# Where VectorE inverts the softmax sums inside a batch element, and where TensorE ranks the tokens: cross-attention with a routed feed-forward layer, Trainium2

## The chip, the cores and the metric

The kernel runs on one core of one Trainium2 chip. The metric is the device time of one execution in microseconds (us), median of the runs shown. Data is float32; the products are made of three products of rounded and rest parts (high x high, high x low, low x high), which TensorE takes as fp32r.

## The reference, cut to what matters

Eight batch elements of 112 tokens of width 512 attend, with 16 heads of 32, to 375 context rows: the first 257 are image rows and the last 118 are text rows, each with its own keys, values and softmax. Then a feed-forward layer of 8 experts follows, of which each token takes its two best.

```python
def attention(q, k, v):
    scores = jnp.einsum('bqhd,bkhd->bhqk', q, k) * scale
    probs = jax.nn.softmax(scores, axis=-1)
    return jnp.einsum('bhqk,bkhd->bqhd', probs, v)

q     = rms_norm(linear(x, q_w, q_b), norm_q_w)                  # x is layer-normed
k     = rms_norm(linear(ctx_txt, k_w, k_b), norm_k_w)
k_img = rms_norm(linear(ctx_img, k_img_w, k_img_b), norm_k_img_w)
x1    = x + linear(attention(q, k_img, v_img) + attention(q, k, v), o_w, o_b)
gate  = softmax(layernorm(x1) @ Wg + bg); topv, topi = top_k(gate, 2)
out   = x1 + sum over the two experts of topv * (gelu(gelu(h @ W1 + b1) @ W2 + b2) @ W3 + b3)
```

## The kernel before, in words

**Bodies and slots.** The five engines (and SyncE for the transfers) run programs of their own, tied by semaphores. After a start (`first()`) come nine bodies b = 0 to 8. Body b attends element b (`has_heads`, b up to 7), prepares queries, keys and values of element b + 1 (`has_prep`, b up to 6), projects and norms element b - 1 (`has_tail`, from b = 1) and routes element b - 2 (`has_route`, from b = 2). b = 7 is LAST, b = 8 is DONE. Then the experts run in blocks of 256 and 128 rows. A body is a loop over 16 slots h, written out in Python for each engine (`body`, lines 1009, 710, 560 and 1332): what an engine does in a slot is an `if` in that list, and the order of the ifs is the order of its queue. Nothing is reordered later, so an instruction that waits holds back all that stands behind it.

**Attention of a head.** Every fourth slot TensorE makes the scores of four heads (`score`, 12 matmuls at L1281). VectorE takes their maxima (`maxima`, L897 and L898, two pairs). ScalarE exponentiates head h in slot h with the row sums beside it (`weigh`, L658 and L660). VectorE inverts the two sums of head h - 1 in slot h (`invert_sums`, L900: a reciprocal at L904 of 112x2 numbers, then a product at L906 over the 118 text columns). ScalarE multiplies the 257 image columns in slot h (`normalise(b, h - 1)`, L666), and waits for the reciprocal alone. TensorE transposes head h - 2 in slot h (`transpose`, L1291, waits for both products and for the bank), ScalarE copies the result out (`take_transposed`, L674). In slots 6, 10, 14 and 2 of the next body TensorE multiplies four heads with the values (`attend`, L1314), and VectorE takes the sum (`attended`, L912).

**Around it, on VectorE.** `normalise_keys` (L836, L837, 257 and 118 columns), `normalise_queries` (L873), the rest parts of keys and queries (`split_keys_low` L887, `split_queries_low` L891) and of the context (`split_ctx_low` L813: 1032 columns in slot 15, 472 in slot 1), key biases (`take_kx` L861), the rest of x (`take_x` L851), layer norms (L816, L819, L823), and the gate: `gate_weights` (L927 to L931, slot 1), `gate_choice` (L936 to L946, slot 2; it ends with the mask `msk`), `gate_slots` (L951 to L955, slot 3).

**On GpSimd.** Rounded parts: `split_queries` (L466), `split_keys` (L459), both of the next element in slot 14 and right behind them `split_ctx_high` (L476, 1032 columns, which waits until ScalarE has taken the values tile v1 out, L641); `attended_high` (L470), x + bias (L577, slot 3), squares (L452), and `scatter` (two indirect DMAs, L534, slot 4).

**On TensorE.** Large products fill each slot (`FILL`): k (L1176 to L1178), kt and qt (L1241 to L1243), v (L1258 to L1260), o (L1265 to L1267). `rank` (L1329, L1330) counts, from `msk`, how many tokens before a token chose the same expert; it stands in slot 3 between the transpose and the second half of kt. It writes the bank pvb, which `gate_slots` must have read (`rank_read`) before the transposes kx (L1203, slot 4) write it. Those need `take_kx` before the transposes xT (L1203, slot 5) write the same bank, and these need `take_x` before attend. The logits (L1360, slot 15) need the `attended` of slot 14, and the second half of v2 stands behind them.

```python
if h == 0 and has_tail(b):          # VectorE, L1013
    invert_sums(b - 1, NH - 1)
if h and has_heads(b):
    invert_sums(b, h - 1)
if h == (6 if fixed(b, DONE) else 3) and has_route(b):   # TensorE, L1362
    pe.wait_ge(S["a_done"], NC * b)
    rank(b - 2)
```

## Time and profile before

| | |
|---|---|
| time, median of 3 runs | 835.34 us (834.56 to 838.92) |
| the profiled execution's own time | 834.9 us |
| its span | 832.7 us |
| busy share: TensorE, VectorE, ScalarE, GpSimd | 93%, 72%, 59%, 29% |
| mean granted TensorE clock | 0.982 |
| start | up to 39 us |
| bodies 0 to 8 | about 39 to 400 us |
| experts | the rest |
| ScalarE waiting for reciprocals (L666 for L904) | 60.6 us in 60 waits |

How to read it: in the page and the views times are us from the start of the span. A row of the timeline is start, duration, engine, line, operation, output<-input, and in brackets how long the engine sat idle before it and what ended that. PE is TensorE's matmuls, PEld its weight loads, DVE VectorE, ACT ScalarE, POOL GpSimd. PEclk is the granted TensorE clock as a part of 2.4 GHz. The spans of matmuls are modelled at their ends, so two that run one behind the other overlap a little in the rows.

### The profile page before, as it was taken

The page shows a single profiled execution, that of the slowest core. Times are in us where ns is not written, and L with a number is a line of the kernel's source. Part 1 is how long each engine was busy: PE and PEld are TensorE (multiplying, and loading weights), DVE is VectorE, ACT ScalarE, POOL GpSimd, SP SyncE. Part 2 cuts the span into 40 slices and gives each one's busy share as a digit, 9 for nine tenths or more (in the row PEclk, how much of TensorE's full clock was granted, in tenths as well). Part 3 has the DMA queues.
Part 4 walks back from the last instruction along what each step waited for, and adds up shares of the span by engine and source line. Part 5 has one row for each costly group of instructions (what it writes and reads, how often), then busy time and mean ns, then how long its engine had stood idle before and what let it go on. Part 6 is the DMA issues. An engine that isn't in the chain of part 4 may idle for free.

```text
span 832.7 us, 17460 instructions
## 1 busy us (share of the span) xinstructions
PE 770.6 (93%) x5995; PEld 666.4 (80%) x5995; DVE 599.6 (72%) x1269; ACT 490.9 (59%) x1136; POOL 240.4 (29%) x302
## 2 busy tenths in 40 slices
PE   4889898999999989787899999999999999999994
PEld 3667676767676767555798999999999999999993
DVE  6767878787978787776676757676676758676664
ACT  4377777767676777786245555554545555554543
POOL 3523334342434333223300505032140505032010
PEclk9989999999999999999999999999999999999998
DMA  9820102011020201142756665748566665648561
GB/s 308 291 83 4 56 6 58 38 35 61 24 72 13 83 13 35 31 175 89 260 203 223 233 232 208 248 172 285 191 248 220 238 233 210 250 172 286 194 220 64
DMA packets 29205, 126.28 MB, mean 152 GB/s; under 512 B 4204, under 2 KB 4220, under 8 KB 19424
## 3 DMA queue, kind: packets, MB, share of 16 engines
q1 hardware_dynamic: 23696, 109.80, 37.6%
q0 software_dynamic: 5456, 15.81, 5.3%
q8 instruction: 29, 0.48, 0.2%
q14 instruction: 24, 0.20, 0.1%
HBM read 108.42 MB, written 18.74 MB: 153 GB/s over the span
## 4 chain that ended last, share of the span: by engine, by line
PE 71%; DVE 11%; ACT 10%; issue 4%; DMA 1%; POOL 0%; SPq 0%; ACTq 0%; DVEq 0%; POOLq 0%
PE tiles L1176 6%; PE tiles L1178 6%; PE tiles L1177 6%; PE scores L1478 4%; PE scores L1480 4%; PE scores L1479 4%; PE ptb L1291 4%; PE pvb L1178 3%; PE pvb L1177 3%; PE ptb L1177 3%; PE pvb L1176 3%; PE ptb L1176 3%; PE ptb L1178 3%; PE scores L1281 2%; ACT scr L658 2%
## 5 line engine op out<-in xcount | busy, mean ns | idle before, releaser
L920 DVE TENSOR_TENSOR w<-scr,w 128x2048 fp32r<-128x2048 f32 x75 | 170.8, 2288 | 59.5 <-ACT w L684 59.5
L684 ACT ACTIVATE w<-scr 128x2048 fp32r<-128x2048 f32 x76 | 144.8, 1909 | 54.8 <-PE scores L1480 54.8
L514 POOL DMA_INDIRECT out_dram<-scr,tok x17 | 18.0, 1058 | 298.7 <-DVE scr L1155 296.2
L666 ACT ACTIVATE scr<-scr,rsum 112x257 f32<-112x257 f32 x128 | 66.7, 521 | 60.6 <-DVE rsum L904 60.6
L1176 PE MATMUL tiles<-w 128*128 128x256 f32 (+1 forms) x288 | 82.9, 288 | 0.6
L1176 PE MATMUL tiles<-c,w 128*128 128x258 f32 (+2 forms) x272 | 79.3, 291 | 2.6 <-DVE c L1129 1.2
L1177 PE MATMUL tiles<-w 128*128 128x256 f32 (+1 forms) x288 | 81.2, 282 | 0.0
L1178 PE MATMUL tiles<-w 128*128 128x256 f32 (+1 forms) x288 | 81.2, 282 | 0.0
L1143 DVE CAST w<-scr 128x256 fp32r<-128x256 f32 (+1 forms) x144 | 41.9, 291 | 52.5 <-ACT scr L774 52.5
L1178 PE MATMUL tiles<-c,w 128*128 128x258 f32 (+2 forms) x272 | 76.9, 283 | 0.0
L1177 PE MATMUL tiles<-c,w 128*128 128x258 f32 (+2 forms) x272 | 76.7, 282 | 0.0
L1291 PE MATMUL ptb<-ident,scr 112*128 112x112 f32 x384 | 61.6, 270 | 15.1 <-ACT scr L674 14.0
L1291 PEld LDWEIGHTS ptb<-ident,scr 112*128 112x128 f32 x384 | 43.0, 143 | 39.6 <-ACT scr L666 24.1
L674 ACT ACTIVATE scr<-ptb 128x336 f32<-128x336 f32 x128 | 57.7, 451 | 24.7 <-PE ptb L1291 24.6
L774 ACT ACTIVATE scr<-tiles,b12s 128x256 f32<-128x256 f32 (+1 forms) x72 | 32.3, 460 | 60.6 <-PE tiles L1178 60.5
L658 ACT ACTIVATE scr<-scores,nmax 112x257 f32<-112x257 f32 x128 | 62.5, 488 | 5.2 <-DVE nmax L898 5.2
L1145 DVE TENSOR_TENSOR w<-scr,w 128x256 fp32r<-128x256 f32 (+1 forms) x144 | 59.4, 413 | 5.0
L1176 PEld LDWEIGHTS tiles<-w 128*128 128x128 f32 x288 | 55.1, 191 | 3.3 <-DVE w L1145 2.3
L897 DVE TENSOR_REDUCE nmax<-scores 112x2 f32<-112x514 f32 x64 | 43.9, 686 | 19.1 <-PE scores L1281 19.1
L1176 PEld LDWEIGHTS tiles<-c,w 128*128 128x128 f32 x272 | 52.0, 191 | 4.4 <-issue 3.3
L1177 PEld LDWEIGHTS tiles<-w 128*128 128x128 f32 x288 | 55.2, 192 | 0.0
L1178 PEld LDWEIGHTS tiles<-w 128*128 128x128 f32 x288 | 55.2, 192 | 0.0
(223 smaller groups left out, 2332.0 us busy)
## 6 DMA issues: line engine op xcount, KB each, us to landing
scr<-in_dram SPq DMA_DIRECT2D x76, 1024.0 KB, 4.9
scr<-in_dram SPq DMA_DIRECT2D x8, 750.0 KB, 4.6
scr<-slots_d SPq DMA_DIRECT2D x10, 528.0 KB, 5.4
scr<-in_dram SPq DMA_DIRECT2D x10, 512.0 KB, 8.8
slots_d<-rows SPq DMA_DIRECT2D x8, 528.0 KB, 11.1
xn<-in_dram SPq DMA_DIRECT2D x9, 256.0 KB
xb<-in_dram SPq DMA_DIRECT2D x8, 224.0 KB, 2.7
xr<-in_dram SPq DMA_DIRECT2D x8, 224.0 KB, 2.6
```

What stands on the lines that cost most here:

```text
L658: act.activation(probs[0:L, s, 0:IMG], scores[0:L, s, 0:IMG], ACT.Exp, bias=nmax[0:L, g, s, 0:1], accum_out=sums[0:L, g, s, 0:1])
L666: act.activation(probs[0:L, s, 0:IMG], probs[0:L, s, 0:IMG], ACT.Copy, scale=rsum[0:L, g, s, 0:1]).then_inc(S["normal_img"], 1)
L674: act.activation(probT[:, h % 8, :, :], ptb[:, 0:KT * L].rearrange("p (t q) -> p t q", t=KT), ACT.Copy).then_inc(S["pt_done"], 1)
L684: act.activation(EH[slot], raw[slot], ACT.Copy).then_inc(S["eh_done"], 1)
L897: dve.tensor_reduce(of[:, :, 0], scores[0:L, 2 * i:2 * i + 2, 0:IMG], AX.X, ALU.max, negate=True)
L920: dve.tensor_tensor(EL[slot], raw[slot], EH[slot].bitcast(F32), ALU.subtract).then_inc(S["el_done"], 1)
L1143: dve.tensor_copy(hH[lay][:, c, 0:n], gel[:, m % 4, 0:n]).then_inc(S["hh_done"], 1)
L1145: dve.tensor_tensor(hL[lay][:, c, 0:n], gel[:, m % 4, 0:n], hH[lay][:, c, 0:n].bitcast(F32), ALU.subtract).then_inc(S["hl_done"], 1)
L1176: pe.matmul(out, wh, xh, start=start, stop=False)
L1177: pe.matmul(out, wh, xl, start=False, stop=False)
L1178: return pe.matmul(out, wl, xh, start=False, stop=stop)
L1291: mm = pe.transpose(ptb[:, t * L:(t + 1) * L], probs[0:L, h % 4, t * P:(t + 1) * P], ident[0:L, 0:L])
```

## The change

VectorE's `invert_sums` leaves its fixed place (head h - 1 at the head of slot h). Heads 0, 4, 8, 9 and 12 keep slot and place; the others go earlier: 1 to the end of slot 1's products (behind the low half of the context), 2 into slot 2 behind `attended`, 3 to the head of slot 3, 5 into slot 5 between `take_kx` and `take_x`, 6 into slot 6 ahead of `attended`, 7 into slot 6 behind `take_o`, 10 into slot 10 ahead of the squares, 11 to the head of slot 11, 13 into slot 13 between `normalise_queries` and `normalise_keys`, 14 into slot 14 behind `attended`, and 15 into slot 15 between `ln_apply` and `split_ctx_low` instead of the next body's slot 0. `gate_slots` goes from slot 3 to slot 4 behind the maxima, TensorE's `rank` in slot 3 behind the second half of kt (in DONE both stay), and GpSimd's `scatter` from slot 4 to slot 5. No instruction is added or taken out, and ScalarE's program is untouched.

```diff
+INVERT_FIRST = {1: 0, 3: 3, 5: 4, 9: 8, 10: 9, 11: 11, 13: 12}
+INVERT_MIDDLE = {6: 6, 10: 10}
@@ gpsimd, body @@
-                    if h == (8 if fixed(b, DONE) else 4) and has_route(b):
+                    if h == (8 if fixed(b, DONE) else 5) and has_route(b):
...
                         scatter(b - 2)
@@ vector, body @@
-                    if h == 0 and has_tail(b):
-                        invert_sums(b - 1, NH - 1)
-                    if h and has_heads(b):
-                        invert_sums(b, h - 1)
+                    if h in INVERT_FIRST and has_heads(b):
+                        invert_sums(b, INVERT_FIRST[h])
                     if h % 4 == 0 and has_heads(b):
                         maxima(b, h // 4, 0)
                         maxima(b, h // 4, 1)
...
                     if h in KEYS_LOW_AT and has_heads(b):
                         split_keys_low(b, p, KEYS_LOW_AT[h])
+                    if h in INVERT_MIDDLE and has_heads(b):
+                        invert_sums(b, INVERT_MIDDLE[h])
...
                     if h in (7, 11, 15) and has_heads(b):
                         attended_low(b, (h - 7) // 4)
+                    if h == 14 and has_heads(b):
+                        invert_sums(b, 14)
                     if h in KEYS_AT and (has_prep if h > 1 else has_heads)(b):
...
                     if h == 2 and has_tail(b):
                         attended(b - 1, 3)
+                    if h == 2 and has_heads(b):
+                        invert_sums(b, 2)
...
                     if h == 1 and has_prep(b):
                         split_ctx_low(b + 2, 1)
+                    if h == 1 and has_heads(b):
+                        invert_sums(b, 1)
                     if h == 5 and has_prep(b):
                         take_kx(b, p)
+                    if h == 5 and has_heads(b):
+                        invert_sums(b, 5)
+                    if h == 5 and has_prep(b):
                         take_x(b)
                     if h == 6 and has_tail(b):
                         take_o(b)
+                    if h == 6 and has_heads(b):
+                        invert_sums(b, 7)
+                    if h == 6 and has_tail(b):
...
                         ln_stats(b, x1, st2, mv2, "ln2")
...
                     if h == 13 and has_prep(b):
                         normalise_queries(b, p)
+                    if h == 13 and has_heads(b):
+                        invert_sums(b, 13)
+                    if h == 13 and has_prep(b):
                         normalise_keys(1 - p, 0)
...
                     if h == 15 and has_prep(b + 1):
                         ln_apply(b + 3, xb[0:L, :], xb, mv1, rs1, "ln1", "xn_done")
+                    if h == 15 and has_heads(b):
+                        invert_sums(b, 15)
+                    if h == 15 and has_prep(b + 1):
                         split_ctx_low(b + 3, 0)
...
-                    if h == (7 if fixed(b, DONE) else 3) and has_route(b):
+                    if h == (7 if fixed(b, DONE) else 4) and has_route(b):
                         gate_slots(b - 2)
@@ tensor, body @@
-                    if h == (6 if fixed(b, DONE) else 3) and has_route(b):
+                    if h == 6 and fixed(b, DONE):
                         pe.wait_ge(S["a_done"], NC * b)
                         rank(b - 2)
...
                     if b in BUSY_AT and h in BUSY_AT[b]:
                         keep_busy(tile_use("o", DONE if fixed(b, LAST) else LAST)[0], BUSY_AT[b][h])
+                    if h == 3 and has_route(b) and not fixed(b, DONE):
+                        pe.wait_ge(S["a_done"], NC * b)
+                        rank(b - 2)
```

## Rows read from the trace of the kernel before

**Rows 1.** Waits from 75 to 400 us: us in total, times, longest.
```profile
ACT scr L666 <- DVE rsum L904: 58.3, 57, 2.2
```

**Rows 2.** Windows: slots 12 to 15 of bodies 1 to 4. Busy us per engine, then granted clock, DMA.
```profile
114.59:126.43 11.84, 10.77 (x91) 7.91 (x90) 9.82 (x30) 8.45 (x28) 4.47 (x7) 1.00 0.04 4
157.84:170.85 13.01, 11.93 (x89) 8.56 (x88) 10.99 (x32) 8.46 (x28) 4.47 (x7) 0.90 0.06 20
201.87:214.60 12.73, 11.65 (x89) 8.33 (x89) 10.71 (x31) 8.45 (x28) 4.46 (x7) 0.92 0.06 21
245.86:258.27 12.41, 11.35 (x90) 8.14 (x90) 10.39 (x31) 8.45 (x28) 4.47 (x7) 0.95 0.07 20
```

**Rows 3.** Timeline of body 3, TensorE, slots 3 to 5.
```profile
178.73 0.45 PE L1291 MATMUL ptb<-ident,scr 112*128 112x112 f32 x3
...
179.68 0.33 PE L1329 MATMUL pvb<-msk,upper 112*112 112x8 f32 x2 [0.50 <-issue]
...
181.62 0.78 PE L1281 MATMUL scores<-kq 32*112 32x376 f32 x12
...
184.06 0.57 PE L1203 MATMUL pvb<-ident,xn 118*128 118x118 f32 x4
...
185.95 0.57 PE L1203 MATMUL pvb<-ident,xb 112*128 112x112 f32 x4 [0.32 <-DVE scr L861]
```

**Rows 4.** Timeline of body 3, VectorE and GpSimd, slots 2 to 4.
```profile
178.81 0.57 DVE L940 TENSOR_TENSOR sel<-tif,iota 112x16 f32<-112x16 f32 x1
179.41 0.17 DVE L946 TENSOR_TENSOR msk<-sel 112x8 f32<-112x8 f32 x1
...
179.52 1.29 POOL L577 TENSOR_TENSOR xr<-xr,obr 112x512 f32<-112x512 f32 x1
...
179.69 1.20 DVE L906 TENSOR_SCALAR scr<-scr,rsum 112x118 f32<-112x118 f32 x1
...
183.97 0.39 DVE L898 TENSOR_REDUCE nmax<-scores 112x2 f32<-112x236 f32 x1
```

**Rows 5.** Timeline of bodies 2 and 3, slots 13 to 15, TensorE, ScalarE and GpSimd.
```profile
165.37 0.50 POOL L459 CAST kq<-scr 128x376 fp32r<-128x376 f32 x1 [0.20 <-DVE scr L837]
165.42 0.51 ACT L666 ACTIVATE scr<-scr,rsum 112x257 f32<-112x257 f32 x1 [1.36 <-DVE rsum L904]
...
166.16 0.59 ACT L641 ACTIVATE scr<-tiles 128x512 f32<-128x512 f32 x1
...
166.41 0.48 PE L1291 MATMUL ptb<-ident,scr 112*128 112x112 f32 x3 [0.54 <-ACT scr L674]
...
166.89 1.05 POOL L476 CAST c<-scr 128x1032 fp32r<-128x1032 f32 x1 [1.01 <-ACT scr L641]
...
167.33 0.92 PE L1360 MATMUL pvb<-wgs,xr 128*112 128x8 f32 x8 [0.44 <-DVE af L912]
```

**Rows 6.** Timeline of body 2, slots 13 to 15, VectorE.
```profile
164.68 0.63 DVE L837 SCALAR_TENSOR_TENSOR scr<-scr,vec,rms 128x118 f32<-128x118 f32 x1
...
166.40 0.54 DVE L887 TENSOR_TENSOR kq<-scr,kq 128x376 fp32r<-128x376 f32 x1
...
166.86 0.32 DVE L912 TENSOR_SCALAR af<-pvb,vbias 128x112 f32<-128x112 f32 x1
...
167.11 1.11 DVE L836 SCALAR_TENSOR_TENSOR scr<-scr,vec,rms 128x257 f32<-128x257 f32 x1
```

**Rows 7.** Timeline of body 1, slot 3, GpSimd and VectorE.
```profile
93.09 1.31 POOL L577 TENSOR_TENSOR xr<-xr,obr 112x512 f32<-112x512 f32 x1
93.16 1.37 DVE L916 TENSOR_TENSOR a<-af,a 128x112 fp32r<-128x112 f32 x1 [0.89 <-POOL a L470]
```

**Rows 8.** Timeline of the start of body 2, TensorE.
```profile
127.82 0.36 PE L1176 MATMUL tiles<-c,w 128*128 128x258 f32 x1 [0.18 <-DVE c L813]
```

**Rows 9.** Timeline of LAST (body 7), slots 7 and 8.
```profile
362.20 0.45 PEld L1281 LDWEIGHTS scores<-kq 32*112 32x112 f32 x12 [0.36 <-issue]
...
362.98 0.51 ACT L666 ACTIVATE scr<-scr,rsum 112x257 f32<-112x257 f32 x1 [1.57 <-DVE rsum L904]
...
363.79 0.68 DVE L897 TENSOR_REDUCE nmax<-scores 112x2 f32<-112x514 f32 x1
```

## The prediction

> **What bounds the kernel now.** I read the waits of the bodies first. ScalarE stands 58.3 us for reciprocals in 57 waits, 2.2 us at most [rows 1]. That is idle time of ScalarE and not time of the kernel, so for each such wait I went to TensorE's timeline and asked whether TensorE stood too. It mostly did not: slots 8 to 11 run with large products back to back. Where it stands in a body, few things are the cause: the rank in slot 3, and in slots 14 and 15 first the transpose and then the logits. I read the rank in body 3: the transpose of slot 3 starts at 178.73, the rank only at 179.68, since its mask starts at 179.41 [rows 3, 4]. In slot 15 the transpose comes at 166.41 (0.54 idle, an ACT copy that came after a late reciprocal) and the logits at 167.33 (0.44 idle, for `attended`) [rows 5]. Then the windows: slots 12 to 15 take 11.84 us where the clock stays at 1.00, and 13.01, 12.73 and 12.41 where the mean falls to 0.90, 0.92 and 0.95 [rows 2]. In those windows the clock went to its lower level, 1.2 GHz, behind these two pauses. Bodies 5 and 6 end like body 1. So a body is TensorE's work, two or three pauses and sometimes a clock that falls; its start hangs on VectorE's queue, which is full from slot 13 on.
>
> **The change part by part.** All sums are against the profiled execution, 834.9 us with a span of 832.7, 0.44 below the median of 835.34.
>
> *Rank, slots 2 to 4.* With the rank behind kt, kt's second half follows the transpose. The time from 178.73 to the scores at 181.62 is 2.89 us [rows 3], of which transpose, kt and rank are 0.22, 1.55 and 0.38 by their starts (an estimate from the starts in this timeline); so 0.73 is pause. All of it goes if the mask is ready at 180.5. I think it is not quite. The reciprocals of heads 1 and 2 now stand ahead of the gate's choice, and `sel`, a small product of two tensors in SBUF, comes some 0.6 later than 178.81 [rows 4]. There it meets GpSimd's 1.29 us sum L577, as head 2's product does now, which took 1.20 instead of its 0.28 [rows 4]. ScalarE's earlier copy of k1 starts GpSimd 0.4 earlier, so L577 ends at 180.42; sel and mask follow, the rank at 180.8, the scores at 181.2. Gain 0.45; bounds 0.1 (both late) and 0.73. One thing is given back: kx must wait until `gate_slots` has read the rank, and that is now behind the maxima. The last of them starts at 183.97, 2.35 behind the scores [rows 4], and the read ends at +2.9; kx now starts at 184.06, +2.44 [rows 3]. So kx waits 0.48. Most of it is absorbed in the pause that xT has anyway for `take_kx` (0.32 idle, at 185.95 [rows 3]); `take_kx` comes 0.11 later. Net -0.34, in bodies 2 to 6: **-1.7**. The other side of `scatter` in slot 5, two indirect DMAs behind the squares of kx, costs nothing: its slots are read after the bodies; cover gone, it would cost GpSimd some 2 us in slot 6.
>
> *Slots 5 to 12.* ScalarE's multiplications of heads 6, 7, 10 and 11 come 1 to 2 us earlier and ScalarE waits for TensorE's next scores instead. TensorE gains nothing. Head 10's reciprocal now stands ahead of the squares and waits for its exponentials about as long as the squares wait for GpSimd: +0.05 in seven bodies, **+0.35**. Bounds 0 and +0.3 each.
>
> *Slots 13 to 15.* This is the large term. Today the keys' last product ends at 165.31, GpSimd's high part of them runs from 165.37 while VectorE does head 13, and GpSimd then idles 1.01 us until ScalarE has copied v1 out, which starts at 166.16; its 1.05 us cast of the context comes at 166.89, when the low part of the keys (166.40) is done and `attended` has begun (166.86) [rows 5, 6]. What that cast holds up is the next key product: 1.11 instead of 0.48 [rows 6]. In the new order head 13 goes ahead of the keys. ScalarE has its reciprocal 0.95 earlier than at 165.42 [rows 5], copies v1 out 0.95 earlier, and GpSimd's cast is no longer short of v1. The keys come 0.4 later, so their high part runs at about 166.2 to 166.65, and the cast follows on GpSimd at once, while VectorE only now learns that it may make the low part. There is a row of just this: the product L916 waited for GpSimd's cast L470, the next GpSimd sum started at 93.09, VectorE at 93.16, and it took 1.37 us instead of some 0.27 [rows 7]. So the low part ends at 168.0 instead of 166.94, `attended` starts 1.04 later, and the logits with it: TensorE's earlier transpose only lengthens the pause ahead of them, from 0.54 and 0.44 to one of 2.3.
>
> The rule behind this is in the Trainium skill, "SBUF — State Buffer", section "Who interferes with whom": an instruction of VectorE with two SBUF inputs and one of GpSimd that reads SBUF lock each other out, the first to issue keeps the ports to its end. By it the low part L887, which no row shows held up, is held up as L916 is; without it this term would be about +0.3. Rows 7 agree (1.37 us).
>
> Part of it comes back: the key product behind is no longer held up by the cast (0.63), but head 15 now stands ahead of the low context (+0.38). The first k product of the next body waits for that low context already now, 0.18 idle at 127.82 [rows 8], and so goes with it. The maxima stood behind the low context and head 15 and now behind the low context alone. I make the first exponentials of the next body 0.5 later: +0.5 in bodies 1 to 5, +0.7 behind body 0, and +0.3 behind body 6, which has no context to cast: **+3.5**. Bounds per body +0.2 (the cast misses) and +1.04 (nothing comes back).
>
> *LAST.* Without large products a late reciprocal counts. Its rank comes 0.45 earlier as above. Head 6 waits 1.57 us behind the layer norm, and the maxima of heads 8 and 9 start at 363.79 behind heads 6 and 7, though the scores are made from 362.20 on and could be read 0.83 later as in other slots [rows 9]; both heads move ahead, and the maxima start 0.84 earlier in all. **-0.85**; bounds -0.3 and -1.8.
>
> *Clock.* A fall costs 0.6, 0.9 and 1.2 us against 11.82 [rows 2], 0.9 in the mean. Three of six ends had one with pauses of some 1.0; with 2.3 I take two more: **+1.8**; bounds -2.7 (none is left) and +2.7.
>
> Sum: -1.7 + 0.35 + 3.5 - 0.85 + 1.8 = +3.1, so 838.0.
>
> **The rivals.** *Nothing in the way* (no change). The low part of the keys gets in ahead of the cast, and the ends of the bodies cost 0.2 instead of 0.5, with no new fall: -1.7 + 0.35 + 1.0 + 1.0 - 0.85 = -0.2, 834.7. For it: 0.1 us decides who is first; against it: rows 7, where GpSimd was. 0.20.
>
> *The pauses go* (faster). The mask is there at 180.5 and the rank gives 0.62 net, `attended` keeps its time, and the three falls vanish with the shorter pauses: -3.1 - 0.85 - 2.7 = -6.6, 828.3. For it: all sums are ready when they are now inverted. Against it: the logits wait for `attended`, not for a reciprocal. 0.17.
>
> *The logits take the blow* (slower). Place: slot 15 of bodies 1 to 5. The 1.04 us stays whole, since TensorE's v2 stands behind the logits, and all six ends fall to the lower clock: -1.7 + 0.35 + 5 x 1.04 + 1.0 - 0.85 + 2.7 = +6.7, 841.6. It decides from 0.7 us more per end than I take. Against it: the maxima of the next body have slack today of half a microsecond. 0.20.
>
> That the change only moves idle time of ScalarE, and so does nothing, comes to 834.9 and lies in the first case.
>
> **How the numbers follow.** Forecast 0.43, its own range 835 to 840. Half a per cent is 4.2 us, about what a measurement of this kernel can tell from no change. Faster than that: most of the third case, 0.16. Slower: the fourth and a little of the forecast's tail, 0.22. The rest, 0.62. The range of 8 in 10 runs from 831 into the fast case to 842.
>
> **What would show it.** In the changed profile: waits of L666 for L904 well under 30 us; the transpose of slot 3 followed by kt and the rank by the scores, 2.4 instead of 2.9 us apart; kx idle for about 0.5 behind DVE pick; the k low part L887 of slot 14 at 1.4 us or more with L476 beside it; one pause of 2 us ahead of the logits; four or five windows at the lower clock. Wrong would be: L887 at 0.54 everywhere and `attended` no later behind `normalise_queries` than now.

## The result: 1% slower, outside the range

| | before | after |
|---|---|---|
| median of 6 runs | 834.95 us (833.1 to 838.92) | 845.18 us (841.85 to 846.75) |
| ratio | | 1.0097 [1.0073, 1.0121] |
| the profiled execution's own time | 834.9 us | 845.31 us |
| mean granted TensorE clock | 0.982 | 0.968 |

Forecast 838.0, range 831 to 842. The direction of the sum was right, its size was not, and the case that the prediction called "The logits take the blow" (841.6, chance 0.20) had the place right. The page of the changed kernel begins:

```profile
span 843.4 us, 17460 instructions
...
PE 778.9 (92%) x5995; PEld 675.1 (80%) x5995; DVE 603.8 (72%) x1269; ACT 489.4 (58%) x1136; POOL 242.2 (29%) x302
```

TensorE does the same 5995 matmuls and is busy 8.3 us longer than before (770.6), at the lower mean clock of the table. Its idle time grew by 2.4 us.

Waits of the changed kernel from 75 to 400 us (us in total, times, longest):

```profile
ACT scr L669 <- DVE rsum L907: 32.4, 35, 1.8
...
PE pvb L1381 <- DVE af L915: 12.5, 6, 2.2
...
PEld pvb L1224 <- DVE pick L954: 3.6, 5, 0.7
...
DVE kq L890 <- POOL kq L462: 2.8, 7, 0.4
```

(L669 for L907 was L666 for L904 before; lines of VectorE moved by 3, of TensorE by 21.) The change did what it says: ScalarE's wait for reciprocals fell from 58.3 us [rows 1] to 32.4 (the prediction had said well under 30). No stretch of the table below got clearly shorter by it. In its place the logits (L1381) wait 12.5 us for `attended`, 2.2 in each of bodies 1 to 5 and 1.41 in body 6. Before, these six waits were 2.6 together. The wait of L890 for GpSimd (L462) occurs at seven body ends, 0 to 6.

Windows of slots 12 to 15, bodies 1 to 6 (busy us per engine, then granted clock, DMA share, GB/s):

```profile
117.73:130.63 12.90, 10.58 (x89) 7.99 (x89) 10.10 (x31) 8.36 (x28) 4.41 (x7) 1.00 0.01 4
161.47:176.32 14.85, 12.53 (x89) 9.43 (x88) 11.20 (x31) 8.45 (x28) 4.41 (x7) 0.85 0.07 17
207.28:220.59 13.31, 10.99 (x89) 8.12 (x88) 10.51 (x31) 8.46 (x28) 4.41 (x7) 0.96 0.06 18
251.58:264.81 13.23, 10.92 (x89) 8.06 (x88) 10.43 (x31) 8.45 (x28) 4.42 (x7) 0.97 0.06 13
295.79:308.90 13.11, 10.80 (x90) 7.99 (x90) 10.32 (x31) 8.45 (x28) 4.41 (x7) 0.98 0.05 11
339.83:351.90 12.07, 10.56 (x90) 7.99 (x89) 8.04 (x27) 8.45 (x28) 3.19 (x5) 1.00 0.04 7
```

The first row is body 1 at full clock: 12.90 against 11.84 [rows 2], the wait alone. The last is body 6, also at full clock: 12.07 against 11.82. In bodies 2 to 5 a fall of the clock comes on top and runs on into the next body. How the wait arises stands in the timeline of body 3, slots 14 and 15, and the start of body 4:

```profile
214.66 0.59 ACT L644 ACTIVATE scr<-tiles 128x512 f32<-128x512 f32 x1
...
215.15 0.45 PE L1312 MATMUL ptb<-ident,scr 112*128 112x112 f32 x3
...
215.21 0.83 POOL L462 CAST kq<-scr 128x376 fp32r<-128x376 f32 x1 [0.79 <-DVE scr L840]
...
215.99 1.04 POOL L479 CAST c<-scr 128x1032 fp32r<-128x1032 f32 x1
216.07 1.36 DVE L890 TENSOR_TENSOR kq<-scr,kq 128x376 fp32r<-128x376 f32 x1 [0.39 <-POOL kq L462]
217.35 0.32 DVE L915 TENSOR_SCALAR af<-pvb,vbias 128x112 f32<-128x112 f32 x1
...
217.82 0.92 PE L1381 MATMUL pvb<-wgs,xr 128*112 128x8 f32 x8 [2.22 <-DVE af L915]
...
219.15 0.39 PE L1281 MATMUL tiles<-w,c 128*119 128x512 f32 x1
...
220.04 0.63 PE L1281 MATMUL tiles<-w,c 128*119 128x512 f32 x1
```

v1 is copied out (L644) before GpSimd is done with the keys, so its context cast L479 follows at once at 215.99, and VectorE's low part, which waited for the keys' high part, comes 0.08 later and takes 1.36 us instead of 0.54 [rows 6]. `attended` (L915) then waits, and the two pauses of 0.54 and 0.44 [rows 5] are one of 2.22. Behind it the clock falls to 1.2 GHz at 219.8: the same large matmul (L1281) goes from 0.39 to 0.63 us. The 1.36 is there at six body ends, those of bodies 0 to 5, in both profiles of the changed kernel. Body 6 has no context to cast: there L890 takes 0.55 and the logits have one pause of 1.41. An L890 that is held up by the cast is what the Trainium skill, "SBUF — State Buffer", section "Who interferes with whom", says of two inputs of VectorE beside a reading GpSimd; the trace agrees (1.36 us beside the cast, 0.55 without).

**Where the 10 us are.** Time from one scores row to another, with the time at the lower clock (granted 0.50) between 75 and 425 us. "Again" is a second profile of the same kernel, on another chip; the other rows are experiments that follow.

| profile, us | bodies 0, 1 | bodies 2 to 6 | LAST, slots 0 to 11 | at lower clock |
|---|---|---|---|---|
| before | 87.0 | 217.8 | 25.7 | 17 |
| before, again | 87.1 | 218.0 | 28.5 | 27 |
| after | 91.2 | 221.3 | 28.6 | 41 |
| after, again | 89.8 | 221.5 | 28.5 | 38 |
| e1, head 13 back | 88.8 | 217.8 | 29.4 | 31 |
| e2, head 13 alone | 91.3 | 222.6 | 26.4 | 34 |
| e3, rank alone | 87.1 | 215.7 | 28.2 | 24 |
| e4, filled | 88.5 | 218.1 | 27.3 | 14 |
| e5, cast later | 90.8 | 221.8 | 29.0 | 41 |
| e14, cast later, filled | 88.9 | 216.1 | 25.7 | 17 |
| e7, before, filled | 87.9 | 216.6 | 28.3 | 17 |
| e9, rank and heads 6, 7 | 87.4 | 212.6 | 27.5 | 24 |
| e10, e9 filled | 87.6 | 212.4 | 28.5 | 17 |
| e13, e9 with heads 1, 2 | 87.1 | 216.0 | 29.1 | 27 |
| e11, e9 filled behind | 87.8 | 211.3 | 26.6 | 10 |
| e12, LAST filled too | 87.0 | 211.4 | 24.8 | 7 |

### The profile page after: what moved, and what is told of

It reads as the page before. It is cut to its first block, busy times and chain, and to the rows that moved or that the text cites. A ratio compares the mean times of both kernels' runs of the same rounds, so it can differ in the third digit from the quotient of the medians.

```text
span 843.4 us, 17460 instructions
## 1 busy us (share of the span) xinstructions
PE 778.9 (92%) x5995; PEld 675.1 (80%) x5995; DVE 603.8 (72%) x1269; ACT 489.4 (58%) x1136; POOL 242.2 (29%) x302
## 4 chain that ended last, share of the span: by engine, by line
PE 72%; DVE 12%; ACT 8%; issue 3%; DMA 2%; POOL 1%; SPq 0%; ACTq 0%; DVEq 0%; POOLq 0%
PE tiles L1197 7%; PE tiles L1199 6%; PE tiles L1198 6%; PE scores L1504 4%; PE scores L1503 4%; PE scores L1502 4%; PE ptb L1312 4%; PE pvb L1199 3%; PE pvb L1198 3%; PE ptb L1198 3%; PE pvb L1197 3%; PE ptb L1197 3%; PE ptb L1199 3%; PE scores L1302 3%; PE pvb L1335 2%
## 5 line engine op out<-in xcount | busy, mean ns | idle before, releaser
L669 ACT ACTIVATE scr<-scr,rsum 112x257 f32<-112x257 f32 x128 | 67.7, 529 | 33.2 <-DVE rsum L907 33.2
L1197 PE MATMUL tiles<-c,w 128*128 128x258 f32 (+2 forms) x272 | 81.3, 299 | 3.9 <-DVE c L816 1.8
L1198 PE MATMUL tiles<-c,w 128*128 128x258 f32 (+2 forms) x272 | 78.4, 288 | 0.0
L1199 PE MATMUL tiles<-c,w 128*128 128x258 f32 (+2 forms) x272 | 78.3, 288 | 0.0
L1312 PE MATMUL ptb<-ident,scr 112*128 112x112 f32 x384 | 63.6, 277 | 8.7 <-ACT scr L677 6.6
L1312 PEld LDWEIGHTS ptb<-ident,scr 112*128 112x128 f32 x384 | 45.0, 147 | 31.8 <-ACT scr L669 13.0
L1197 PEld LDWEIGHTS tiles<-c,w 128*128 128x128 f32 x272 | 53.9, 198 | 5.5 <-issue 3.6
L1197 PEld LDWEIGHTS tiles<-w 128*128 128x128 f32 x288 | 55.1, 191 | 3.3 <-DVE w L1166 2.3
L455 POOL TENSOR_TENSOR scr<-scr 128x257 f32<-128x257 f32 (+1 forms) x40 | 29.6, 743 | 89.9 <-ACT scr L653 57.4
L1198 PEld LDWEIGHTS tiles<-w 128*128 128x128 f32 x288 | 55.2, 192 | 0.0
## 6 DMA issues: line engine op xcount, KB each, us to landing
slots_d<-rows SPq DMA_DIRECT2D x8, 528.0 KB, 11.6
```

What stands on the lines that cost most here:

```text
L669: act.activation(probs[0:L, s, 0:IMG], probs[0:L, s, 0:IMG], ACT.Copy, scale=rsum[0:L, g, s, 0:1]).then_inc(S["normal_img"], 1)
L1197: pe.matmul(out, wh, xh, start=start, stop=False)
L1198: pe.matmul(out, wh, xl, start=False, stop=False)
L1199: return pe.matmul(out, wl, xh, start=False, stop=stop)
L1312: mm = pe.transpose(ptb[:, t * L:(t + 1) * L], probs[0:L, h % 4, t * P:(t + 1) * P], ident[0:L, 0:L])
```

## The experiments

Each run is compared with runs of the kernel before on the same chip. In none is any of the computation left out; "filled" ones have idle matmuls more, whose products nobody reads.

**e1: head 13 goes back behind the keys.** The whole change but one entry.

```diff
-INVERT_FIRST = {..., 13: 12}
+INVERT_FIRST = {..., 13: 12, 14: 13}
@@ slot 13 @@
-                    if h == 13 and has_heads(b):
-                        invert_sums(b, 13)
```

> The changed kernel with head 13 alone put back to the head of slot 14, behind the first key product. Theory A (the early head 13 lets GpSimd's context cast run right behind its key cast, so VectorE's low part of the keys is locked out, the logits come 1 us later, and the longer pause brings the clock down): the low part of the keys in slot 14 is back at 0.54 us from 1.36, the logits start some 40.5 us behind the body's first scores instead of 41.5, there are no more falls of the clock than before the change, and the time is 832 to 836. Theory B (the cost lies in the other moves: head 15 ahead of the context's low part, the rank and kx): the time stays above 841. In between, 837 to 841, both have a share.

840.87 us, ratio 1.0026 [1.0009, 1.0043]. The time lies between the two theories, where both have a share. The low part of the keys is back to 0.54 at all ends, and the logits come 9.49 us behind the scores of slot 12 (after: 10.54, before: 9.49). Three ends have a fall (bodies 2, 3 and 6), as many as before. Slots 0 to 3 of a body with a start at full clock take 11.02 us where before took 10.99: of the rank's gain nothing is left. Bodies 0 and 1 still take 1.8 us more than before, though the low part of the keys is not late. The first k product of body 1 waits in one long pause, and the clock falls at 89.6 behind it:

```profile
88.17 0.36 PE L1194 MATMUL tiles<-c,w 128*128 128x258 f32 x1 [1.82 <-DVE c L816]
```

**e2: head 13 alone**, in the kernel before.

```diff
-                    if h and has_heads(b):
+                    if h and h != 14 and has_heads(b):
                         invert_sums(b, h - 1)
@@ slot 13, between normalise_queries and normalise_keys @@
+                    if h == 13 and has_heads(b):
+                        invert_sums(b, 13)
```

> The kernel before with one thing changed: head 13 is inverted between the queries and the keys in slot 13. Theory A: the low part of the keys takes about 1.36 us, the logits start 1 us later, and the time is 840 to 846, since this alone carries the loss. Theory B: within 2 us of before, 833 to 837.

847.9 us, 1.0116 [1.0095, 1.0137], above the 840 to 846 that were expected. One reciprocal and its product, moved ahead of two keys' products, cost as much as the whole change. The low part takes 1.36 us at the ends of bodies 0 to 5 and 0.55 at that of body 6, and the clock falls at four of six ends. Slots 0 to 3 of body 5, which starts at full clock, take 10.45 us instead of 10.99: half a microsecond of the late logits comes back though the rank stands where it stood.

**e3: the rank alone**, with `gate_slots` and `scatter`; no reciprocal moves.

```diff
-                    if h == (7 if fixed(b, DONE) else 3) and has_route(b):
+                    if h == (7 if fixed(b, DONE) else 4) and has_route(b):
                         gate_slots(b - 2)
@@ tensor, body; the old place of rank is kept for DONE alone @@
...
@@ tensor, body, behind kt of slot 3 @@
+                    if h == 3 and has_route(b) and not fixed(b, DONE):
+                        pe.wait_ge(S["a_done"], NC * b)
+                        rank(b - 2)
```

> The kernel before with only the rank, gate_slots and scatter moved as in the change. Theory A: the rank part is a small gain; the mask is there at its old time, so nearly all of the 0.73 us pause goes and 0.1 to 0.5 comes back at kx: 831 to 834. Theory B: kx behind the maxima gives it all back and more, 836 to 840.

838.03 us, 0.9989 [0.997, 1.0008]. The second scores come 0.8 us earlier, but slots 8 to 11 take 10.66 instead of 9.99: the transpose of head 6 now waits 0.6 for its reciprocal, which stands behind the layer norm in slot 7. Half a gain, handed back four slots later.

**e4: nine idle matmuls ahead of the logits**, in the changed kernel: the wait stays, the pause goes.

```diff
+                    if h == 15 and has_tail(b) and has_prep(b):
+                        bank, cnt = tile_use("k0" if has_prep(b + 1) else "o", b + 1)
+                        pe.wait_ge(tile_free[bank], cnt)
+                        keep_busy(bank, 9)
```

> The changed kernel with nine 512-column matmuls into a free bank between the transpose and the logits of slot 15, bodies 1 to 6; they do no work for the output and fit into the pause of about 2.4 us. Theory A with the clock as its second step: the waits stay (logits 41.5 us behind the first scores), the clock does not fall behind them, and the time drops from 845 to 836 to 840. Rival C (the wait for the logits costs the time and the clock costs next to nothing): 843 to 846.

843.47 us, 1.007 [1.0042, 1.0097]; the profiled execution, at 840.41, is the fastest of four (granted clock 0.986, the others 0.976 to 0.981). In it there is no fall in bodies 2 to 6, slots 12 to 15 take 12.90 in bodies 2 to 5 (12.53 in body 6), and each of bodies 2 to 5 takes 43.67 to 43.73. A body of before without a fall takes 42.95 or 43.04, so the wait costs 0.65 a body by itself (1.06 in slots 12 to 15, of which some 0.45 comes back in slots 0 to 3). The median lies in the range that was named for the clock costing next to nothing, and it gained only 0.3% on the changed kernel, inside the two intervals: this run shows what the wait costs, not what the clock costs.

**e5: GpSimd's context cast one slot later**, behind `attended_high`.

```diff
-                    if h == 14 and has_prep(b + 1):
+                    if h == 15 and has_prep(b + 1):
                         split_ctx_high(b + 2, 0)
```

> The changed kernel with every inversion where the change put it, and only GpSimd's context cast of slot 14 moved behind attended_high of slot 15, so that it can no longer follow the key cast at once. Theory A (the lock-out by that cast): the low part of the keys in slot 14 is back at 0.54 us, the logits start within 0.5 us of where they did before the change (40.4 to 41.0 behind the first scores), and the ratio to before is 0.997 to 1.004. Theory B (what costs is that head 13 stands ahead of the keys and delays their chain by itself): the logits stay a full microsecond late and the ratio stays at 1.007 or more.

845.45 us, 1.0083 [1.0045, 1.0122], a miss: 0.997 to 1.004 was expected. Its timeline, end of body 3:

```profile
213.61 0.83 POOL L462 CAST kq<-scr 128x376 fp32r<-128x376 f32 x1 [0.79 <-DVE scr L840]
...
214.47 0.55 DVE L890 TENSOR_TENSOR kq<-scr,kq 128x376 fp32r<-128x376 f32 x1 [0.39 <-POOL kq L462]
...
215.42 0.92 PE L1381 MATMUL pvb<-wgs,xr 128*112 128x8 f32 x8 [1.41 <-DVE af L915]
215.56 1.87 POOL L479 CAST c<-scr 128x1032 fp32r<-128x1032 f32 x1
```

The low part takes 0.55 again and the logits are 9.74 behind the scores of slot 12, 0.25 later than before: the wait is gone, the time is not. The window of slots 12 to 15 of body 3 (body 2 takes 13.10 too):

```profile
205.68:218.78 13.10, 11.59 (x89) 8.54 (x88) 10.30 (x31) 8.46 (x28) 5.24 (x7) 0.91 0.07 20
```

The clock falls to 1.2 GHz at every end of bodies 2 to 6, in the profile for 3.41 us from 172.2, 216.6, 260.9, 305.3 and 349.7. At the end of body 1 there is the same pause (1.42) and no fall. The pauses of before, 0.54 and 0.44 with matmuls between them, are together 0.98; here there is one of 1.41.

**e14: e5 with five idle matmuls in that pause**, as in e4 but `keep_busy(bank, 5)`.

> The changed kernel with the context cast of GpSimd put behind attended_high of slot 15 (as in the run of the cast put later, which took VectorE's context copy back to 0.55 us, put the logits only 0.25 us later than before, and was still 0.8% slower, with the clock at .50 for 3.41 us at every body end), and 5 idle matmuls of TensorE between the transposition of slot 15 and the logits, where its one pause of 1.41 to 1.45 us was. If the falls of the clock are what it lost: no fall at the ends of bodies 1 to 6, last quarters of about 12.1 us, bodies of 43.0 to 43.4 us, and 0.998 to 1.003 of the time of before. If the loss is a wait of the new order that has nothing to do with the clock: the bodies stay at 44 us or more and the ratio at 1.006 or more.

838.1 us (12 runs), 1.0021 [1.0011, 1.0032]. The profiled execution, at 835.08, is the fastest of the twelve. Its window of body 3:

```profile
202.67:214.74 12.07, 11.74 (x96) 8.81 (x95) 9.32 (x29) 7.94 (x27) 5.24 (x7) 1.00 0.04 9
```

Nothing else was touched, no end has a fall, the logits are as far behind the scores as in e5 (9.73), and bodies went from 44.36 to 43.2 us. So most of what e5 lost at its ends was the clock, shown by this pair: some 1.15 us for a fall of 3.41. (The texts before e14 and a0 call L890 the context copy; it is the low part of the keys.)

**a0: the changed kernel again**, unedited, on e14's chip.

> The changed kernel, not edited, profiled a second time on another chip. If its falls of the clock come from its order of work: a fall at five or six of the ends of bodies 1 to 6, as in the first profile, a span of 840 to 846 us, the context copy of slot 14 on VectorE at 1.36 us at every body end. If their number was the chance of one profile: three or four of the ends, as in the two profiles of the kernel before, and a span of 836 to 840 us.

843.98 us, span 841.9. L890 takes 1.36 at the ends of bodies 0 to 5 again. The clock falls at 88.7, 170.6, 218.4, 262.8, 307.1 and 354.9, in the first profile at 86.7, 172.0, 219.8, 264.2, 308.5 and 356.3: at the start of body 1, at the ends of bodies 2 to 5, and in slots 0 to 3 of LAST. That is four of six ends both times, the one of body 2 for 6.83 us, and not five or six. The kernel before, profiled again (b0, below), had falls at three of six ends, as the first time, but not at the same three. So the places of the falls are this order's, and not the luck of one profile. That it has more of them at the ends rests on four against three.

**e7: the kernel before, filled**: two idle matmuls ahead of the transpose of slot 15 and two ahead of the logits.

```diff
+                    if h == 15 and has_tail(b) and has_prep(b):
+                        bank, cnt = tile_use("k0" if has_prep(b + 1) else "o", b + 1)
+                        pe.wait_ge(tile_free[bank], cnt)
+                        keep_busy(bank, 2)
@@ behind the transpose @@
+                    if h == 15 and has_tail(b) and has_prep(b):
+                        keep_busy(tile_use("k0" if has_prep(b + 1) else "o", b + 1)[0], 2)
```

> The kernel before with two idle matmuls ahead of the transpose and two ahead of the logits of slot 15, in bodies 1 to 6, inside the two pauses of TensorE; nothing else. If the falls of the clock at the ends of bodies come from these pauses, they are gone and their 0.6 to 1.2 us each with them: ratio 0.994 to 0.998. If they come from something else, or the fillers get in the way: 0.999 to 1.003.

836.4 us, 0.9997 [0.9978, 1.0015]. No fall in bodies 1 to 6, but slots 12 to 15 take 12.57 each: the first filler waited 0.92 to 0.94 us for ScalarE (L641) to free the bank. Clock gained, wait added.

**e9: the parts that should pay**: the rank as in e3, and heads 6 and 7 as in the change, ahead of `attended` and of the layer norm. All other heads as before.

```diff
-                    if h and has_heads(b):
+                    if h and h not in (7, 8) and has_heads(b):
                         invert_sums(b, h - 1)
@@ slot 6, ahead of attended @@
+                    if h == 6 and has_heads(b):
+                        invert_sums(b, 6)
@@ slot 6, behind take_o @@
+                    if h == 6 and has_heads(b):
+                        invert_sums(b, 7)
```

> The kernel before with the rank part of the change and, of the inversions, only heads 6 and 7 early (slot 6). The trace of the rank part alone showed the second scores 0.8 us earlier in a body and then 0.69 us lost at the transpose of head 6, whose reciprocal stands behind the layer norm. Theory A: with head 6 early that loss is gone, slots 8 to 11 take 9.99 us again, a body is 0.5 us shorter, LAST about 0.8: ratio 0.993 to 0.997. Theory B (the gain is taken back elsewhere): 0.998 to 1.002.

832.05 us, 0.9952 [0.9937, 0.9967]: faster than before. Slots 0 to 3 take 9.91 to 10.45 (10.15 where the clock stays up), slots 8 to 11 10.0. Slot 3 of body 4 (its scores start at 211.59), TensorE and GpSimd:

```profile
220.45 1.30 POOL L577 TENSOR_TENSOR xr<-xr,obr 112x512 f32<-112x512 f32 x1
...
221.34 0.27 PE L1334 MATMUL pvb<-msk,upper 112*112 112x8 f32 x2
...
221.74 0.78 PE L1286 MATMUL scores<-kq 32*112 32x376 f32 x12
```

The rank has no idle time ahead of it. Its mask was ready at 220.50, when L577 had only begun.

**e13: e9 with heads 1 and 2 early as in the change.**

```diff
-                    if h and h not in (7, 8) and has_heads(b):
+                    if h and h not in (2, 3, 7, 8) and has_heads(b):
                         invert_sums(b, h - 1)
@@ slot 2, behind attended @@
+                    if h == 2 and has_heads(b):
+                        invert_sums(b, 2)
@@ slot 1, behind split_ctx_low @@
+                    if h == 1 and has_heads(b):
+                        invert_sums(b, 1)
```

> The kernel with the rank part and heads 6 and 7 early (e9_rank_and_6_7), and heads 1 and 2 early as well, as the change has them, ahead of the gate's weights and choice. Theory A (they push the gate's mask behind the second half of kt, so the rank waits again): the pause ahead of the rank, gone in e9, is back at 0.5 us or more, the first quarter of a body is 10.5 us or more instead of 10.0 to 10.2 where the clock stays up, and the ratio to before is 0.998 to 1.002 against 0.995 for e9. Theory B (the two heads cost nothing): like e9, 0.993 to 0.997.

837.38 us, 1.0008 [0.9989, 1.0027]: the gain of e9 is gone, and slots 0 to 3 take 10.97 to 10.99 where the body starts at full clock. Slot 3 of body 4 (scores at 213.60):

```profile
222.06 1.29 POOL L577 TENSOR_TENSOR xr<-xr,obr 112x512 f32<-112x512 f32 x1
...
222.14 1.24 DVE L938 CAST tif<-topi 112x2 f32<-112x2 uint32 x1
...
223.41 0.41 DVE L940 TENSOR_TENSOR sel<-tif,iota 112x16 f32<-112x16 f32 x1
223.85 0.17 DVE L946 TENSOR_TENSOR msk<-sel 112x8 f32<-112x8 f32 x1
...
224.12 0.33 PE L1338 MATMUL pvb<-msk,upper 112*112 112x8 f32 x2 [0.60 <-issue]
```

Two reciprocals with their products ahead of the gate's choice bring its cast `tif` beside L577, where it takes 1.24 us instead of 0.17. So `sel` starts behind the end of L577, and the rank waits 0.60 again.

**e10: e9 with e7's fillers.**

> The one before with the four idle matmuls of slot 15 as well. If the two gains are independent, both ratios multiply: 0.988 to 0.995. If the clock falls elsewhere instead, it is no better than without them.

832.75 us, 0.996 [0.9942, 0.9977]: the same as e9; the bank's wait ate what the clock gave.

**e11: e9 with two fillers only between the transpose and the logits**, where the bank is already free.

> e9_rank_and_6_7 with two idle matmuls between the transpose and the logits of slot 15 only; the two ahead of the transpose are left out, since in e7 they waited for ScalarE to free the bank and made the end of each body 0.75 us longer. If the falls of the clock at the ends of bodies hang on the sum of the two pauses, they are gone with one of them filled, and slots 12 to 15 take 11.82 us in every body: ratio 0.991 to 0.995. If they still come, as e9: 0.994 to 0.997.

831.85 us, 0.9943 [0.9918, 0.9968]. Slots 12 to 15 take 11.82 to 11.85 in bodies 2 to 6, no fall, bodies of 42.25. The gain over e9 (0.9952) is inside the intervals: the profiles show it, the medians do not.

**e12: e11 with more fillers in LAST.**

```diff
-BUSY_AT = {LAST: {h: 2 for h in range(1, 16)}, DONE: ...
+BUSY_AT = {LAST: {**{h: 2 for h in range(1, 16)}, 1: 10, 3: 4, 9: 9, 13: 7, 15: 5}, DONE: ...
```

> e11 with more idle matmuls in LAST's pauses (slots 1, 3, 9, 13, 15), where the clock fell in every version so far. If LAST's length is the clock's, its quarters go from about 9.5, 9.3, 8.7 to at most 9.5, 7.6, 7.3 and the ratio to 0.988 to 0.993. If it is the chain of exponentials, no more than 0.5 us is won against e11.

829.49 us, **0.9909 [0.9888, 0.993]**, the best; its interval overlaps e11's. End of body 3, TensorE:

```profile
208.31 0.48 PE L1296 MATMUL ptb<-ident,scr 112*128 112x112 f32 x3 [0.55 <-ACT scr L674]
208.71 0.72 PE L1327 MATMUL tiles<-w 128*128 128x512 f32 x2
209.27 0.88 PE L1369 MATMUL pvb<-wgs,xr 128*112 128x8 f32 x8
```

The first pause of before is still there (0.55); only the second one is filled, and the logits are not later.

**b0: the kernel before, profiled again**, on the chip of e11 to e13.

> The kernel before itself, unchanged, for a second profile on another chip. Both theories: quarters of bodies as in the first profile where the clock stays up (10.95, 10.28, 9.99, 11.82); the falls of the clock may sit at the ends of other bodies, 2 to 4 of the six. If all six ends fell or none, the comparison with the changed kernel's falls would rest on chance.

838.2 us, span 836.0. Its first eight slots of LAST, and those of the changed kernel:

```profile
344.10:355.85 11.75, 8.55 (x59) 5.50 (x58) 8.27 (x30) 6.98 (x27) 1.85 (x4) 0.65 0.26 92
355.85:364.87 9.02, 9.02 (x69) 6.62 (x68) 4.54 (x13) 5.59 (x22) 2.76 (x4) 0.82 0.74 284
```

```profile
351.90:362.48 10.58, 7.82 (x59) 5.22 (x58) 7.83 (x27) 7.35 (x27) 2.08 (x4) 0.70 0.27 91
362.48:371.78 9.30, 9.30 (x69) 6.81 (x68) 5.29 (x19) 6.11 (x24) 2.87 (x4) 0.79 0.78 304
```

The long fall at the start of LAST is in the kernel before too, in one of its two profiles, and there costs as much. What the first two profiles differ by in slots 0 to 7 is therefore not shown to be the change's.

## Why the prediction was wrong, step by step

**The end of the body: right in mechanism and size.** L890 was to take what L916 took, 1.37: measured 1.36, six times of six, at the ends of bodies 0 to 5. `attended` and logits 1.04 later: measured 1.05. That half a microsecond of it comes back in the next body: 0.45, from e4. The term of +3.5 comes to the whole 1.06 in body 1, 0.6 in each of bodies 2 to 5 and some 0.25 given back in body 6, in all some 3.2.

**The rank: sized at -1.7, it gave nothing.** The prediction put the rank at 180.8, 9.95 behind the body's first scores. In the changed kernel it is at 10.06 in body 2:

```profile
138.19 0.45 PE L1312 MATMUL ptb<-ident,scr 112*128 112x112 f32 x3
...
140.69 0.33 PE L1350 MATMUL pvb<-msk,upper 112*112 112x8 f32 x2 [0.65 <-DVE msk L949]
141.15 0.78 PE L1302 MATMUL scores<-kq 32*112 32x376 f32 x12
```

so the row was read nearly right, and the sum of slots 0 to 3 falls from 10.99 to 10.52. But this 0.47 is the same half microsecond that the end-of-body term had already taken back: with the logits on time (e1) those slots take 11.02, and with the logits late and the rank unmoved (e2) 10.45. The failed step is "Net -0.34, in bodies 2 to 6": it added two savings that end at one wait, the mask. e3 and e9 (10.15 and 10.16 where the clock stays up) show what the move is worth without heads 1 and 2 ahead of the gate's choice, 0.8 a body; e13 shows that these two take all of it. The prediction had seen them push `sel` by 0.6, and had `sel` meet L577; what met it is the cast ahead of `sel` (1.25, body 2) or the mask behind it (1.21 to 1.24, bodies 3 to 6).

It also named 2.4 us from the transpose of slot 3 to the scores; body 2 has 2.96, bodies 3 to 6 about 2.3, because there the start at the lower clock brings TensorE to the mask later. Body 6, VectorE and TensorE:

```profile
317.76 1.22 DVE L949 TENSOR_TENSOR msk<-sel 112x8 f32<-112x8 f32 x1
...
319.08 0.33 PE L1350 MATMUL pvb<-msk,upper 112*112 112x8 f32 x2
```

The rank is 10.18 behind the scores (308.90) there: a fall in slot 0 is partly hidden, since the mask and not TensorE sets the rank. The wait of kx for `gate_slots` came as foreseen (3.6 us in five, above).

**Slots 5 to 12: right.** +0.3 in bodies 1 to 6 (10.03 to 10.06 against 9.99), forecast +0.35.

**The clock: sized at +1.8, and the start of body 1 left out.** The prediction counted falls of two ends more at 0.9. It was one end more, four instead of three, with one fall twice as long: against e4's fall-free 43.67 they cost some 3.6 us, before's three against 43.0 some 2.8, so +0.8. What was not looked at was the start of body 1. There are no logits in body 0, so the delay goes to the next thing in VectorE's queue. The changed kernel, VectorE:

```profile
82.20 1.36 DVE L890 TENSOR_TENSOR kq<-scr,kq 128x376 fp32r<-128x376 f32 x1 [0.40 <-POOL kq L462]
...
85.82 1.23 DVE L816 TENSOR_TENSOR c<-scr,c 128x1032 fp32r<-128x1032 f32 x1
```

and TensorE, of the changed kernel and then of the kernel before:

```profile
83.82 0.78 PE L1302 MATMUL scores<-kq 32*112 32x376 f32 x12 [0.82 <-DVE kq L890]
...
87.19 0.56 PE L1197 MATMUL tiles<-c,w 128*128 128x258 f32 x1 [1.81 <-DVE c L816]
```

```profile
85.06 0.48 PE L1291 MATMUL ptb<-ident,scr 112*128 112x112 f32 x3 [0.60 <-ACT scr L674]
86.28 0.36 PE L1176 MATMUL tiles<-c,w 128*128 128x258 f32 x1 [0.74 <-DVE c L813]
```

The first k product starts 0.91 later behind one pause of 1.81, the clock falls for 6.83 us from 86.7, and slots 0 to 3 of body 1 take 13.72 instead of 10.78. That is the place where the forecast's own sentence ("the first k product waits for that low context already now", rows 8) applied with the larger +0.7, but without a clock. Bodies 0 and 1 cost 4.2 us in the first pair of profiles, 2.7 in the second (there the fall lasts 3.41 us). The late low part of the keys is not the only cause: in e1, without it, the pause is 1.82 and the clock falls too. Of the moves that e1 keeps, head 15 stands ahead of L816; it was not tried alone.

**LAST: -0.85 had the wrong sign in its second half.** Heads 6 and 7 did let the maxima start 1.04 behind the scores (372.82 against 371.78) instead of 1.59 [rows 9], a gain of 0.55 where 0.84 was forecast (the rows give 1.59 less 0.83, so 0.76 at most). But slots 8 to 11 take 8.73 instead of 7.75. TensorE there, in the changed kernel and in the kernel before:

```profile
371.78 0.77 PE L1302 MATMUL scores<-kq 32*112 32x376 f32 x12
...
373.63 0.48 PE L1312 MATMUL ptb<-ident,scr 112*128 112x112 f32 x3 [0.15 <-ACT scr L677]
...
376.43 0.64 PE L1312 MATMUL ptb<-ident,scr 112*128 112x112 f32 x3 [1.84 <-ACT scr L677]
```

```profile
363.97 0.48 PE L1291 MATMUL ptb<-ident,scr 112*128 112x112 f32 x3 [0.99 <-DVE scr L906]
...
367.41 0.48 PE L1291 MATMUL ptb<-ident,scr 112*128 112x112 f32 x3 [1.37 <-ACT scr L674]
```

Pauses of 0.99 and 1.37 became 0.15 and 1.84: less in sum, but the clock falls for 3.41 us behind the 1.84. It is so in every profile with these two heads early (8.54 to 8.74, e11 9.52), and in none of before, e2 and e7 without them (7.75 to 7.77); e3 is the exception, below. e12, which fills that pause, has no fall there and takes 8.03. The rest of LAST, slots 0 to 7, is +1.9 in the first pair of profiles and -1.0 in the second.

**The sum again**, from the first pair of profiles: rank 0, squares +0.3, ends +3.2, bodies 0 and 1 beside the wait +3.1, clock of bodies 2 to 6 +0.8, LAST +2.9: 10.3 beside the 10.4 between the profiled executions. How much of it is clock in all is less sure. Over the 84 executions of the kernel before that stood beside the experiments (four chips), the time falls by 4.6 us for each 0.01 of mean granted clock (correlation -0.80), with 0.978 in the mean; the six of the changed kernel have 0.969. By that slope some 4 us are clock (an estimate: the slope is that of another order of work). The 8.3 us that TensorE is busy longer in the profiled pair point to more, so the split between clock and waits is not settled.

Of the rivals, "Nothing in the way" and "The pauses go" fell with L890. "The logits take the blow" came nearest; it had all six ends fall where four did, and was short by the rank, by body 1's start and by LAST.

**What stays open.** Why the clock falls at some ends of the kernel before and not at others, and why not at the end of body 1 of the changed kernel, behind the same pause of 2.2 us, in either profile. Whether one long pause brings the fall or the longer sum of pauses: at the ends the one of e5 is longer (1.41) than the two of before together (0.98). Whether slots 0 to 7 of LAST are slower by the change. Why e3, without early heads, took 10.61 us in slots 8 to 11 of LAST, with a fall of 6.83 us; its profile has a pause of 1.81 ahead of head 6's transpose, where before has 0.99. How much of e14's last 0.2% lies in bodies 0 and 1 (1.9 us more than before in its profile) was not tried apart.

## What to carry to other kernels

An instruction moved to where its input is "just there" still stands in a queue, and the cost is what it meets: here keys that came 0.4 us later let GpSimd's cast in ahead, and the logits were 1.05 us late. Count a saving once per wait that it ends at; two savings ahead of one late mask are one. And look at where pauses of TensorE will merge, the first body too: one pause of 1.41 us in place of two of 0.98 together brought falls that cost more than the wait, and five idle matmuls in it took the ratio from 1.0083 (e5) to 1.0021 (e14). Where the bank was not yet free, such matmuls made a wait of their own (e7, e10).

## What the runs showed of the hardware that was not expected

- One pause of 1.41 us was followed by a fall at five of six ends (e5); two of 0.54 and 0.44, with three matmuls between them, at three of six, in both profiles of the kernel before. TensorE is busy 11.6 of 13.1 us in the windows of e5. A pause of 2.2 us in the changed kernel was not always followed by one: at four of five ends.
- e5's bodies 3 to 6 are 44.36 to 44.38 us long, the starts of its falls are 44.3 to 44.4 us apart, and each fall is met by the same slots. Without falls (e14) the bodies are 43.2.
- VectorE's L890, waiting for GpSimd's cast of the keys, lost to the next instruction in GpSimd's queue: it started 0.08 us behind (216.07 against 215.99) and took 1.36 instead of 0.54 us, six times of six. `msk`, 112x8 numbers, took 1.22 us beside GpSimd's x + bias (L580 there) instead of 0.17, and `tif`, 112x2 numbers, 1.24 (e13).
- Moved into slot 15, GpSimd's context cast itself took 1.87 instead of 1.04 us beside VectorE's products (e5).
